# A recurrent-cell weight held in HBM as bf16: one row-major copy against eight column blocks of 128, feeding the DMA transposes

## What is computed

```python
x = x + layernorm(causal_mean(layernorm(x)))            # part 1: running mean over the 4096 rows
h = gelu(concat(layernorm(x), slot_mean) @ w1 + b1)      # part 2: routing
alpha = softmax over the top 8 of (h @ w2 + b2) / (|tau| + 0.1)
si = (alpha^T @ layernorm(x)) / (sum(alpha) + 1e-8)      # 64 x 1024
gi = si @ Wih.T + bih                                    # part 3: a GRU cell on 64 slots
gh = S  @ Whh.T + bhh                                    # Wih, Whh: 3072 x 1024, float32
r, z = sigmoid(i_r + h_r), sigmoid(i_z + h_z)
n = tanh(i_n + r * h_n);  S_new = (1 - z) * n + z * S
# attention over the 64 slots (wq, wk, wv), layernorm, @ wvp -> slot_values
out = layernorm((alpha @ slot_values) @ wo + bo);  x = x + out
```

## Time and profile before

| | us |
|---|---|
| median of the two timed runs | 844.64 (842.42 to 846.86) |
| the profiled execution, its own time | 843.31 |
| its span on the slowest core (core 0), first to last instruction | 841.8 |
| spans of the 8 cores | 834.4 to 841.8 |
| PE busy / DVE busy / ACT busy / POOL busy | 341.2 / 343.0 / 275.9 / 163.2 |

### The profile page before, as it was taken

One profiled execution on the slowest core, in us unless ns is written; L12 is line 12 of the kernel. 1 busy time (PEld: TensorE's weight loads), 2 busy tenths in 40 slices (PEclk: granted clock), 3 DMA queues, 4 the chain that ended last, 5 costly groups with the idle time before them and its releaser, 6 DMA issues.

```text
span 841.8 us, 6996 instructions; the slowest of 8 cores (834.4 to 841.8 us)
## 1 busy us (share of the span) xinstructions
PE 341.2 (41%) x1724; PEld 128.9 (15%) x1737; DVE 343.0 (41%) x1049; ACT 275.9 (33%) x344; POOL 163.2 (19%) x91
## 2 busy tenths in 40 slices
PE   0002354353363361787786225662222474222220
PEld 0001000000010001344443113221221121000000
DVE  0003525525525437744621102554002104888883
ACT  0001342342343435556753203771001111323322
POOL 2001242242242242000000002000000002556564
PEclk9999555555555555788997555555555576555555
DMA  7998999998993001000000552003452331234224
GB/s 192 247 265 234 100 122 103 108 117 100 121 104 50 0 2 37 1 1 1 1 2 0 110 114 41 0 2 75 113 123 75 115 100 50 101 124 175 100 116 184
DMA packets 69287, 76.29 MB, mean 91 GB/s; under 512 B 53216, under 2 KB 57312, under 8 KB 68640
## 3 DMA queue, kind: packets, MB, share of 16 engines
q0 software_dynamic: 4800, 22.25, 23.4%
q1 hardware_dynamic: 64448, 53.60, 21.4%
HBM read 68.72 MB, written 36.70 MB: 125 GB/s over the span
## 4 chain that ended last, share of the span: by engine, by line
DVE 31%; PE 30%; DMA 10%; ACT 9%; issue 9%; another core or an unknown queue 8%; DVEq 1%; POOLq 0%; ACTq 0%; SPq 0%; POOL 0%
DVE bn6x L192 11%; PE p_h L564 8%; DVE tmp L173 7%; DVE bn6c L192 5%; DMA whhT<-whh_bf 4%; DMA whhT<-wih_bf 4%; PE pcs L406 4%; PE pcs L414 3%; ACT x1b L207 2%; PE ptot L418 2%; PE p_si L678 2%; PE pcs L410 2%; ACT x2bf L207 2%; PE p_gi L801 1%
## 5 line engine op out<-in xcount | busy, mean ns | idle before, releaser
L207 ACT ACTIVATE stat<-stat 128x2 f32<-128x2 f32 (+1 forms) x64 | 13.1, 204 | 295.2 <-DVE stat L184 293.4
L432 POOL TENSOR_TENSOR sb_x<-anb,sb_x 128x1024 f32<-128x1024 f32 x32 | 74.3, 2340 | 164.9 <-ACT anb L207 164.9
L1158 POOL TENSOR_TENSOR sb_x<-fnb,sb_x 128x1024 f32<-128x1024 f32 x32 | 74.2, 2337 | 70.4 <-ACT fnb L207 70.4
L192 DVE BATCH_NORM_STATS2 bn6c<-pcs 128x6 f32<-128x512 f32 x64 | 39.9, 686 | 116.9 <-PE pcs L414 111.6
L406 PE MATMUL pcs<-x1b,s_tri 128*128 128x512 bf16 x61 | 31.6, 615 | 132.1 <-ACT x1b L207 131.8
L192 DVE BATCH_NORM_STATS2 bn6x<-sb_x 128x6 f32<-128x512 f32 x128 | 77.5, 678 | 0.0
L564 PE MATMUL p_h<-x3t,sb_w1a 128*128 128x512 bf16 x248 | 69.7, 450 | 14.7 <-DVE bn6x L192 7.5
L1109 PE MATMUL p_f<-sb_sv,sb_alphaT 64*128 64x512 bf16 x64 | 30.1, 577 | 84.6 <-ACT fnb L207 76.1
L207 ACT ACTIVATE x2bf<-sb_x,stat 128x1024 bf16<-128x1024 f32 x32 | 36.4, 1137 | 52.3 <-PE p_at L684 52.3
L207 ACT ACTIVATE x3b<-sb_x,stat 128x1024 bf16<-128x1024 f32 x32 | 37.9, 1233 | 46.1 <-DVE stat L173 27.1
L192 DVE BATCH_NORM_STATS2 bn6x<-p_f 128x6 f32<-128x512 f32 x64 | 39.9, 686 | 11.2 <-PE p_f L1109 10.9
(11 more groups left out here) (170 smaller groups left out, 505.5 us busy)
## 6 DMA issues: line engine op xcount, KB each, us to landing
sb_x<-x SPq DMA_DIRECT2D x8, 2048.0 KB, 38.7
out<-sb_x SPq DMA_DIRECT2D x8, 2048.0 KB, 6.6
whh_bf<-Whh POOLq DMA_DIRECT2D x1, 6144.0 KB, 61.5
wih_bf<-Wih POOLq DMA_DIRECT2D x1, 6144.0 KB, 118.1
wv_bf<-wv POOLq DMA_DIRECT2D x1, 2048.0 KB, 145.3
wvp_bf<-wvp POOLq DMA_DIRECT2D x1, 2048.0 KB, 163.6
wo_bf<-wo POOLq DMA_DIRECT2D x1, 2048.0 KB, 178.5
wst<-wv_bf SPq DMA_DIRECT2D x8, 256.0 KB, 3.3
```

The lines of the kernel that those rows point to most:

```text
L192: return gv.emit([out], [a], lambda: v_.bn_stats(out, a))
L207: lambda: s_.activation(out, in_, func, bias=bias, scale=scale, accum_out=accum))
L432: g.tensor_tensor(sb_x[:, j * D:(j + 1) * D], anb[:, (j % 3) * D:(j % 3 + 1) * D], sb_x[:, j * D:(j + 1) * D], op=OP.add).then_inc(sX2, 1)
L1158: g.tensor_tensor(sb_x[:, j * D:(j + 1) * D], fnb[:, (j % 4) * D:(j % 4 + 1) * D], sb_x[:, j * D:(j + 1) * D], op=OP.add).then_inc(sX5, 1)
```

## The change

The bf16 copies of `Whh` and `Wih` get another shape: instead of 3072 x 1024, row by row, they are eight blocks of 3072 x 128, one per column chunk, one behind the other. POOL issues 8 DMAs for each of the two, each reading 3072 runs of 128 float32 (512 bytes, one every 4096 bytes) and writing 3072 x 128 bf16 (3072 runs of 256 bytes, back to back). SP's 16 transposes read a contiguous block of 786,432 bytes instead of 3072 pieces of 256 bytes that stand 2048 bytes apart. `semGh` and `semGw` now count to 128. Everything else is the same, and so is the order of POOL's list: the 16 DMAs stand where the two stood, ahead of the other five copies and of the 32 additions.

```diff
-    whh_bf = nc.dram_tensor("whh_bf", [G3, D], BF16, kind="Internal").ap()
-    wih_bf = nc.dram_tensor("wih_bf", [G3, D], BF16, kind="Internal").ap()
+    whh_bf = nc.dram_tensor("whh_bf", [8 * G3, P], BF16, kind="Internal").ap()
+    wih_bf = nc.dram_tensor("wih_bf", [8 * G3, P], BF16, kind="Internal").ap()
@@ POOL
-                g.dma_start(out=whh_bf, in_=w_d["Whh"]).then_inc(semGh, 16)
-                g.dma_start(out=wih_bf, in_=w_d["Wih"]).then_inc(semGw, 16)
+                for cc in range(8):
+                    g.dma_start(out=whh_bf[cc * G3:(cc + 1) * G3, :],
+                                in_=w_d["Whh"][:, cc * P:(cc + 1) * P]).then_inc(semGh, 16)
+                for cc in range(8):
+                    g.dma_start(out=wih_bf[cc * G3:(cc + 1) * G3, :],
+                                in_=w_d["Wih"][:, cc * P:(cc + 1) * P]).then_inc(semGw, 16)
@@ SP
-            s.wait_ge(semGh, 16)
+            s.wait_ge(semGh, 128)
...
                 s.dma_start_transpose(whhT[:],
-                                      whh_bf[:, dc * P:(dc + 1) * P]).then_inc(semWT[dc], 16)
+                                      whh_bf[dc * G3:(dc + 1) * G3, :]).then_inc(semWT[dc], 16)
@@ SP
-                s.wait_ge(semGw, 16)
+                s.wait_ge(semGw, 128)
...
-                    s.dma_start_transpose(whhT[:], wih_bf[:, dc * P:(dc + 1) * P]).then_inc(semWT[dc], 16)
+                    s.dma_start_transpose(whhT[:], wih_bf[dc * G3:(dc + 1) * G3, :]).then_inc(semWT[dc], 16)
```

## The result

The changed kernel takes 930.3 us (median, 926.1 to 940.7) against 844.1 us: a ratio of 1.101, 95% interval 1.099 to 1.104. The forecast was 919 us, range 868 to 990.

What follows compares the result with a forecast made beforehand. Stage 1 was taken as a ring of engines waiting for each other, stopped by whoever drops out for long. 843.3 us plus 77.5 for POOL's hold minus 2 for transposes gave 919 us, range 868 to 990.

Steps and rivals of the forecast that it cites:

- Transposes: SP's transposes from a contiguous source: 2 us gained, as packets stay 256 bytes; at most 11 us by the rows.
- The copies' DMA time: Draining the 16 column copies: 50 ns a packet, 9.6 us a DMA, 154 us for all, hidden beside stage 1.
- the line through `w2` and `w1`: Packet price interpolated between `w2` packets (33 ns) and `w1` packets (106 ns): 44 ns at 256 bytes.
- POOL's issues: POOL's time to issue: 1.83 us per 3072-packet copy, sixteen 29.3 us; by issue time alone nothing is lost.
- Where POOL is held: POOL stands in an issue until earlier copies drain, delaying stage 1's additions: 77.5 us lost, between bounds 0 and 116.
- The step of two thirds: Choice of the hold at POOL's issues between 0 us (room for everything) and 116 us (room for one more): 77.5 us.
- The estimate of room for five: Skill-based: 1024 descriptors an engine hold five copies; POOL free after the eleventh lands, at 192.9 us, 78 us late.
- What is won back: Stage 1: ACT idles 6.8 us at tile 3, so POOL may be late until 115.0 us; after release nothing is won back.
- POOL is not held: Rival at POOL's issues: all sixteen put down in 29 us, copies drain beside stage 1; 841 us, chance 0.12.
- Quicker transposes: Rival: contiguous transposes quicker by a third or more and POOL not held; 832 or 830 us, some 820 at best; chance 0.05.
- a double price for short writes: Rival: POOL held and short HBM writes cost double, 100 ns or more a packet; 1014 us (977 milder), chance 0.11.
- the signs named ahead: Signs: issues 1.5 to 2.5 us, then 6 to 12; first addition near 193; ACT idle from 118; stage 1 pace kept.

Runs made afterwards that it cites:

- experiment 1: Against the changed kernel, each of the 16 copies of `Whh` and `Wih` got its own semaphore: 915.5 us, ratio 1.084.
- experiment 2: The changed kernel with half the room for POOL's descriptors (`dynamic_dma_scratch_size=8192`): 937.4 us, ratio 1.110.
- experiment 9: Kernel with two transpose buffers and column-block copies between the additions, plus SP waiting for all 21 copies before any transpose: 805.9 us, ratio 0.950.
- experiment 10: Two transpose buffers, column copies issued early (two before stage 1, two behind each of seven addition pairs), own semaphores, room for three: 807.9 us, ratio 0.952.

## Why the prediction was right, point by point

**Transposes.** Taken: 2 us gained, because each packet stays 256 bytes. Measured: 77.1 us of waits became 77.2. The reason holds, the gain is nothing. The 350 to 400 GB/s that the Trainium skill (DMA: Bandwidth & Descriptors, Latency and other measured facts) gives for the contiguous case do not show up here: the plateau is 288 to 294.

**The copies' DMA time.** Taken: 50 ns a packet, between 44 and 60. Read as the prediction read its rows, the first five copies (80 to 126 us) give 1.114 x 46000 x 16 / 15440 = 53 ns:

```profile
q0 software_dynamic: 15440, 3.93, 111.4%
```

But packets of one engine overlap, and the sum needed the pace at which they drain: 965 packets an engine between 82.3 and 124.9 us, 44 ns each; the next eight copies between 129.6 and 191.7 us, 40 ns each; 43 ns (8.3 us over 193) with own semaphores. So the packet time was met and the pace taken 6 to 10 ns too slow. That the line through `w2` and `w1` gave 44 is in part luck: it goes through packet times, and by that measure the packets cost 9 ns more than the line says. Nothing doubled below 512 bytes. The DMA time stayed hidden: SP's waits for the copies never ended last.

**POOL's issues.** Taken: 1.83 us for 3072 packets, by a slope from the `w1` rows. Measured: 1.29 us (`L291`, 1292 ns), 9 us less in all, inside the time that the hold covers anyway.

**Where POOL is held.** Taken: the first addition possible at 192.5 us, as two thirds between no hold and a hold with room for one copy. Measured: 198.6. Two errors nearly cancel. The packets were cheaper: with a release one by one and 8.3 us a copy it would be the 182.5 of experiment 1. And a release one by one was assumed, where the shared semaphores made it three groups, 16 us later. The step of two thirds was a choice between bounds, and it was luck that it lay near the room of five copies that experiments 1 and 2 show. The estimate of room for five that stood beside it, with the sixteenth copy behind the eleventh, had the mechanism; only its release one by one needs a semaphore for each copy.

**What is won back.** Taken: ACT has 6.8 us of slack behind tile 3. In the changed kernel core 5 takes 411.0 - 201.1 = 209.9 us from the write of tile 3 to the first transpose; before, the same core took 322.3 - 109.4 = 212.9 us (the first number is the first transpose's start, below):

```profile
L483 SPq DMA_TRANSPOSE whhT<-whh_bf x8: 3127/3414/4272, 322.3 to 508.0; - x8
```

So tile 3 is written 91.7 us later, 3.0 us come back in stage 1 and 0.8 behind it: 87.9, which is core 5's span against its own before (929.2 - 841.3). The slack was sized 3.8 us too high.

**The 11 us between forecast and result.** Of the 87.9 us on core 5 the prediction had 77.5 - 2 = 75.5. The later first addition is 6.1 of the difference, the slack 3.8, the transposes 2.

**The rivals.** "POOL is not held" fell with the first gap of 39.6 us. Quicker transposes and a double price for short writes fell with the rows above. Of the signs named ahead, the hold behind the fifth issue, the first addition near 193 us (198.6), the pace of stage 1, the packets and the landings were there. Three were not: the first issues took 1.29 us and not 1.5 to 2.5; ACT stopped at 110 us and not at 118; and the issues after the fifth come in groups, with the time in front of them, instead of at the pace of one drain.

## What to carry to other kernels

A DMA that POOL issues takes room for each of its packets, and a copy cut by columns has one for each short run; before cutting, count the packets that an engine gets and add up what is outstanding, and look at what stands behind those issues in POOL's list. If they must be many, issue them between other work, and give each its own semaphore. And ask what a transfer's time is made of before changing its layout: here it was latency and the same 3104 packets either way. Two buffers hid half of the wait (803 to 808 us), and contiguity did not touch it.

## What the runs showed of the hardware that I had not expected

- The room for POOL's descriptors is given back by semaphore count. Copies that share a semaphore come back only when all outstanding ones on it have landed: holds of 39.6, 23.2 and 32.8 us, against 6 to 8 us each with own semaphores. The DMA engines ran dry twice meanwhile, for 4.7 and 3.9 us.
- Column copies that write 256-byte runs to HBM drain at about the same pace whether the runs are back to back or 2048 bytes apart: the first five at 44 and 42 ns a packet an engine (930.3 and 932.8 us in all).
- Transposes in flight beside copies of large packets are slow out of proportion: 73 to 133 us to land for the second of two in flight, 14.7 us with one, 5.3 us alone, and on two cores PE stood still for 34 to 44 us with nothing named. That the stalls go when transposes and copies are kept apart is shown by experiments 9 and 10. That PE waited for an instruction fetch behind the transpose is suggested by the packets of q8 and q14, not shown.
